# Attention's result stored token by token and turned by a transposing DMA, instead of by TensorE

## The chip, the cores and the metric

One Trainium2 chip, all 8 cores, one launch. Each core takes one of the 8 sequences of the batch with the whole weights; the cores exchange nothing. The metric is the device time of the slowest core, in microseconds.

## The reference

For each sequence of 2048 tokens and 4096 features:

```
x = x + layernorm(attention(layernorm(x)))       # w_in 6144 x 4096, w_out 4096 x 4096
x = x + layernorm(ffn(layernorm(x)))             # sign(weight) 4096 x 4096
```

Attention has 32 query heads and 8 key and value heads of 128 features, rotary embedding, a causal mask and a softmax over the keys; its result, 4096 features per token, is multiplied by `w_out.T`. The second part scales its input and output by a routing softmax over 8 experts and multiplies by the signs of the weights.

## The kernel before

The tokens are handled in four blocks of 512 (tb 0 to 3). An input of a projection lies in SBUF as a block of 128 partitions x 16384 bf16: partition p holds, for each of the 32 groups of 128 features, feature p of the group for 512 tokens. TensorE contracts over partitions, so every projection needs its input turned this way (features on partitions).

**The main line.** `main` walks through `groups`: v, k and q projections for blocks 0 and 1, then q, k and v for blocks 2 and 3, then the output projection ("o") for blocks 0 and 1 and for 2 and 3, then the second part ("f"). A pass of one group over one block is 128 matmuls of 512 columns, yielded in 32 steps of 4. The weights come by GpSimd's queue (`w_load`), 1 MB each, cast on the way, issued as the slot before comes free (`w_next`).

**The sides.** Generators are advanced beside the main line by its step number. Attention over blocks 0 and 1 ("att0") runs beside the q, k, v passes of blocks 2 and 3 (steps 802 to 1512); attention over blocks 2 and 3 ("att1") beside the output projection of blocks 0 and 1 (steps 1538 to 2040). "signs" (steps 802 to 1262) loads the second part's weights (`sgw`), turns them to signs and stores them (`wfs`). All engines work in program order, so this weaving is fixed.

**Attention.** An item is one head and one piece of 128 keys: `scores` makes a matmul into one of two PSUM banks taken in turn (`next_s`), ScalarE's exp reads it into `pt`; 3 items later `values` makes up to 4 matmuls of 129 columns into two banks. At the end of a head `scaled` divides by the sums (VectorE, into `an`: tokens on partitions, 4 x 128 features), and 3 items later `turned` takes a bank of `next_s`, makes 4 TensorE transposes of 128 x 128 (helper line 33) into it, VectorE copies the bank into one of three `ast` buffers (line 65), and the sync queue stores it to `As` in DRAM, 1 KB per partition. There are 128 heads in all (32 heads x 4 blocks).

**The queues around it.** The sync queue (SP) issues, in order: the q tiles' stores (`Qs<-qst`, two buffers, made by the rotary step on VectorE in the q passes), the q tiles' loads three heads ahead (`qb<-Qs`), the stores to `As`, the stores of signs (`wfs<-sgo`), and later `out2s<-o2a`, `x<-xin`, `o<-out2s`. `load_at(tb, over)` loads a block for the output projection from `As` in 4 DMAs of 1 MB (`blk_r<-As`). It is called at steps 1506, 1537, 2018 and 2050 for the blocks 0 to 3; their passes begin at the steps 1537, 1569, 2049 and 2081. A pass takes the quarters of the block in order, 8 steps each.

Of the kernel before, what the change touches and what calls it, by code (L numbers as in the profile page):

```python
# [7 lines left out]
BF16 = mybir.dt.bfloat16  # L8
# [6 lines left out]
E = 4096  # L15
# [12 lines left out]
def f_mm(out, lhsT, rhs, start=True, stop=True):  # L28
    return lambda e: e.matmul(out, lhsT, rhs, start=start, stop=stop)  # L29


def f_tr(out, in_, ident):
    return lambda e: e.transpose(out, in_, ident)  # L33
# [18 lines left out]
def f_tt(out, a, b, op):  # L52
    return lambda e: e.tensor_tensor(out, a, b, op=op)  # L53
# [10 lines left out]
def f_vcopy(out, in_):  # L64
    return lambda e: e.tensor_copy(out, in_)
# [21 lines left out]

def f_dma(out, in_):
    return lambda e: e.dma_start(out=out, in_=in_)  # L89


class Prog:
# [44 lines left out]
    def pe(self, make, waits=(), sig=False):  # L137
        return self.put("tensor", make, waits, "sT" if sig else None, 1)

    def act(self, make, waits=()):  # L140
        return self.put("scalar", make, waits, "sA", 1)

    def dve(self, make, waits=()):
        return self.put("vector", make, waits, "sV", 1)

    def load(self, eng, out, in_, name, waits=()):
        return self.put(eng, f_dma(out, in_), waits, name, 16)
# [49 lines left out]
def build_program():  # L197
    nc = bass.Bass("TRN2", target_bir_lowering=False)
    dt_in = lambda n, s, t: nc.dram_tensor(n, s, t, kind="ExternalInput").ap()
    scr = lambda n, s, t: nc.dram_tensor(n, s, t, kind="Internal").ap()  # L200
# [14 lines left out]
    out = nc.dram_tensor("out", [S, E], F32, kind="ExternalOutput").ap()  # L215

    Qs = scr("Qs", [4, 32, 128, 512], BF16)
    As = scr("As", [4, 128, 32 * 512], BF16)
    out2s = scr("out2s", [S, E], BF16)
    x2s = scr("x2s", [S, E], F32)  # L220
    ys = scr("ys", [1024, E], BF16)
# [3 lines left out]
    K = 1024  # L225
    BASE = 16512
    R0, R1, R2 = BASE, BASE + 32 * K, BASE + 64 * K
# [8 lines left out]
    al = nc.alloc_sbuf_tensor_at  # L236
# [14 lines left out]

    qb = [al(f"qb{i}", [128, 512], BF16, offset=R1 + i * K) for i in range(4)]
    pt = [al(f"pt{i}", [128, 512], BF16, offset=R1 + (4 + i) * K) for i in range(10)]
    an = [al(f"an{i}", [128, 512], BF16, offset=R1 + (14 + i) * K) for i in range(2)]
    rec = [al(f"rec{i}", [128, 4], F32, offset=R1 + (16 + i) * K) for i in range(2)]
    ast = [al(f"ast{i}", [128, 512], BF16, offset=R1 + (24 + i) * K) for i in range(3)]
    o2a = [al(f"o2a{i}", [128, 512], BF16, offset=R1 + (27 + i) * K) for i in range(4)]

    x5 = al("x5", [128, E], F32, offset=R1)
# [11 lines left out]
    o = F0  # L271

    def small(n, shape, t, nbytes):
        nonlocal o
        r = al(n, shape, t, offset=o)
        o += nbytes
        return r

    ident = small("ident", [128, 128], BF16, 256)
# [17 lines left out]
    o = p_end  # L297
# [6 lines left out]
    o = p_end + 2048  # L304
# [6 lines left out]
    p = Prog(nc)  # L311
    pe, act, dve, load = p.pe, p.act, p.dve, p.load
# [7 lines left out]
    def next_s():  # L320
        turn["s"] += 1
        return RB[(turn["s"] - 1) % 2]
# [260 lines left out]
    a_tok = {}  # L583
# [85 lines left out]
    LAG = 3  # L669
    pt_free = [[] for _ in pt]  # L670
    qb_free = [[] for _ in qb]
    an_free = [[], []]
    rec_free = [[], []]
    ast_free = [[] for _ in ast]
    as_tok = {}
    r1_over = [[]]
    att = {"pt": 0}
# [4 lines left out]
    def q_load(k):  # L682
        if k < len(heads):
            n = k % 4
            q_in[k] = load("sync", qb[n][:, :], Qs[heads[k][0], heads[k][1]], f"qb{n}",
                           [q_tok[heads[k]]] + qb_free[n] + r1_over[0])

    def attention(lo, hi):
        if lo == 0:
            for k in range(3):  # L690
                q_load(k)
        items = []
        for k in range(lo, hi):
            tb, h = heads[k]
            for kc in range(4 * tb + 4):
                items.append((k, tb, h, kc, max(0, kc - 4 * tb)))
        todo = {}
        made = {}
        norm = {}

        def scores(it):
            k, tb, h, kc, j = it
            qn = k % 4
            if kc == 0:
                q_load(k + 3)
            c0 = j * 128
            b = next_s()
            s = att["pt"] % len(pt)
            att["pt"] += 1
            ko = (h // 4) * 1024 + (kc % 8) * 128  # L710
            tk = pe(f_mm(b.f[:, c0:512], k_sb[kc // 8][:, ko:ko + 128], qb[qn][:, c0:512]),
                    [q_in[k]] + b.free + k_ready[kc // 8], sig=True)
            qb_free[qn] = [tk]
            col = tb * 32 + h
            ex = act(f_act(pt[s][:, c0:512], b.f[:, c0:512], AF.Exp, bias=qmx[:, col:col + 1], scale=ALPHA),
                     [tk] + pt_free[s] + nb_tok[tb] + r1_over[0])
            b.free = [ex]
            mk = ex
            if kc >= 4 * tb:
                mk = dve(f_tt(pt[s][:, c0:c0 + 128], pt[s][:, c0:c0 + 128], tri[:, :], ALU.mult),  # L720
                         [ex, tc[1]])
            made[k, kc] = (s, ex, mk)

        def values(it):

            k, tb, h, kc, j = it
            s, ex, mk = made.pop((k, kc))
            vo = ((kc % 8) * 8 + h // 4) * VN
            v = v_sb[kc // 8][:, vo:vo + VN]
            tk = None  # L730
            opened = set()
            for n in list(range(j + 1, 4)) + [j]:
                vb = VB[n // 2]
                first = kc == 0 and n // 2 not in opened
                opened.add(n // 2)
                w = [ex] + v_ready[kc // 8]
                if kc == 0:
                    w = w + vb.free
                if n == j:
                    w = w + [mk]  # L740
                tk = pe(f_mm(vb.f[:, (n % 2) * VN:(n % 2 + 1) * VN], pt[s][:, n * 128:(n + 1) * 128], v,
                             first, n % 2 == 1 and kc == 4 * tb + n), w, sig=(n == j))
            pt_free[s] = [tk]
            if kc - 4 * tb in (1, 3):
                scaled(k, (kc - 4 * tb) // 2, tk)

        def scaled(k, m, tk):
            vb = VB[m]
            v3 = vb.f[:, 0:2 * VN].rearrange("p (a b) -> p a b", b=VN)
            rc3 = rec[k % 2][:, 2 * m:2 * m + 2].unsqueeze(2)  # L750
            rc = dve(f_rcp(rc3, v3[:, :, 128:129]), [tk] + rec_free[k % 2])
            nv = dve(f_tt(an[k % 2][:, m * 256:(m + 1) * 256].rearrange("p (a b) -> p a b", b=128),
                          v3[:, :, 0:128], rc3.broadcast_to([128, 2, 128]), ALU.mult),
                     [tk, rc] + an_free[k % 2])
            vb.free = [nv]
            norm[k] = nv

        def turned(k):
            tb, h = heads[k]
            b = next_s()  # L760
            tk = None
            for n in range(4):
                tk = pe(f_tr(b.h[:, n * 128:(n + 1) * 128], an[k % 2][:, n * 128:(n + 1) * 128], ident[:, :]),
                        ([norm[k]] + b.free) if n == 0 else (), sig=(n == 3))
            an_free[k % 2] = [tk]
            rec_free[k % 2] = [norm[k]]
            n = k % 3
            ev = dve(f_vcopy(ast[n][:, :], b.h[:, 0:512]), [tk] + ast_free[n])
            b.free = [ev]
            st = load("sync", As[tb, :, h * 512:(h + 1) * 512], ast[n][:, :], f"as{n}", [ev])  # L770
            ast_free[n] = [st]
            as_tok[tb] = latest(as_tok.get(tb, []), [st])

        for n, it in enumerate(items):
            k, tb, h, kc, j = it
            at_n = n + LAG + max(0, 2 - kc)
            todo.setdefault(at_n, []).append(lambda it=it: values(it))
            if kc == 4 * tb + 3:
                todo.setdefault(at_n + 3, []).append(lambda k=k: turned(k))
        n = 0  # L780
        while n < len(items) or todo:
            if n < len(items):
                scores(items[n])
            for f in todo.pop(n, ()):
                f()
            yield 0.3 + (512 - items[min(n, len(items) - 1)][4] * 128) / 512
            n += 1
# [3 lines left out]

    def load_at(tb, over):
        b = blk[AB[tb]]
        a_tok["o", tb] = [[load("sync", b[:, c * 4096:(c + 1) * 4096], As[tb, :, c * 4096:(c + 1) * 4096],
                                f"at{tb % 2}{c}", as_tok[tb] + over)] for c in range(4)]


    x2_tok = {}
# [356 lines left out]
        r1_over[0] = xuse["x", 1]  # L1155

    def after_attention():
        r1_over[0] = p.now("sT", "sA", "sV", "as0", "as1", "as2", "o2a0", "o2a1", "o2a2", "o2a3")
        x5_free[0] = r1_over[0]
        o5_free[0] = r1_over[0]  # L1160
        f_over[0] = f_over[1] = p.now("sT")
        load_consts()
# [140 lines left out]
```

How the kernel before makes its waits and increments, by code:

```python
        def f(e, make=make, tgt=tgt, pairs=tuple(pairs)):  # L127
            for (h, v) in pairs:
                e.wait_ge(h, v)
            i = make(e)
            if tgt is not None:
                i.then_inc(*tgt)
# [19 lines left out]
    def wait(self, eng, toks):  # L152
        pairs = tuple((self.sem[t[0]][0], t[1]) for t in toks)
        self.q[eng].append(lambda e, pairs=pairs: [e.wait_ge(h, v) for (h, v) in pairs])
```

## Time and profile before

| | us |
|---|---|
| median of 3 runs | 4134.55 |
| the runs | 4120.65 to 4147.13 |
| the profiled execution's own time | 4127.55 |
| its span on the slowest core (core 6) | 4126.0 |
| spans of the 8 cores | 4091.9 to 4126.0 |

The profile is of core 6, one execution. PE is TensorE's matmuls, PEld its weight loads, DVE VectorE, ACT ScalarE, POOL GpSimd, SP the sync queue. A profile's row gives busy time; what bounds the kernel is read from what each engine waited for, in the stretch in question. On core 6, att0 runs from about 818 to 1690 us of the span and att1 from about 1720 to 2573 us.

### The profile page before, as it was taken

What the parts mean: (1) busy time and instruction counts of PE and PEld (TensorE: products, weight loads), DVE (VectorE), ACT (ScalarE), POOL (GpSimd) and SP (SyncE); (2) the same over time, 40 slices, a digit from 0 to 9 for tenths busy, and PEclk for the clock granted to TensorE, in tenths of its full rate; (3) what the DMA queues carried; (4) which work ended last, traced back from release to release, by engine and by line L of the source; (5) the groups of instructions that cost most, each with busy time, mean ns of one, the idle gap of its engine ahead of it and who ended that gap; (6) DMA issues with size and microseconds to landing.
All of it is one profiled execution on the core that took longest, in us unless ns stands there. A gap on an engine that the chain in (4) does not pass through costs nothing.

```text
span 4126.0 us, 61645 instructions; the slowest of 8 cores (4091.9 to 4126.0 us)
## 1 busy us (share of the span) xinstructions
PE 3870.7 (94%) x22113; PEld 1897.1 (46%) x22448; DVE 1722.9 (42%) x3284; ACT 1428.4 (35%) x2293; POOL 171.7 (4%) x327
## 2 busy tenths in 40 slices
PE   5999999988888999999999999989999999999997
PEld 2444444444444454555555555444444434344343
DVE  5155555755544453122211111334345666543444
ACT  2111111144555433366666666222212212121222
POOL 0000000000000000000000000000000000000110
PEclk8999999999999999999999999999999999999999
DMA  9445656588987834633332233885844534267874
GB/s 230 74 86 101 121 101 125 124 163 179 188 165 154 163 65 83 151 75 75 76 70 61 64 70 100 217 186 152 206 110 159 169 106 168 70 196 226 237 252 166
DMA packets 189945, 565.69 MB, mean 137 GB/s; under 512 B 21328, under 2 KB 96208, under 8 KB 160976
## 3 DMA queue, kind: packets, MB, share of 16 engines
q0 software_dynamic: 46512, 269.05, 34.5%
q1 hardware_dynamic: 143136, 292.68, 22.4%
q8 instruction: 187, 3.06, 0.3%
q14 instruction: 110, 0.90, 0.1%
HBM read 620.95 MB, written 142.61 MB: 185 GB/s over the span
## 4 chain that ended last, share of the span: by engine, by line
PE 76%; DMA 12%; DVE 5%; issue 3%; ACT 3%; SPq 1%; DVEq 0%; ACTq 0%; POOL 0%; POOLq 0%
PE ps L29 74%; DMA Qs<-qst 3%; DMA out<-xfc 3%; PE ps L33 2%; ACT pt L37 2%; DMA o<-out2s 2%; DMA wfs<-sgo 1%; DVE bn L77 1%; DMA x<-xin 1%; SPq L89 1%; DMA bia<-bias_in 1%; DMA wsl<-wv 1%; DVE yt L53 1%; DVE yst L53 1%; DVE t L53 0%
## 5 line engine op out<-in xcount | busy, mean ns | idle before, releaser
L29 PE MATMUL ps<-wsl,blk_r 128*128 128x512 bf16 x4982 | 1214.6, 384 | 47.6 <-DMA wsl<-wv 19.9
L29 PE MATMUL ps<-blk_r,wsl 128*128 128x512 bf16 x4986 | 1177.6, 383 | 12.6 <-DVE t L53 5.4
L37 ACT ACTIVATE pt<-ps,qmx 128x512 bf16<-128x512 f32 (+3 forms) x1280 | 763.0, 622 | 650.1 <-PE ps L29 640.3
L29 PEld LDWEIGHTS ps<-blk_r,wsl 128*128 128x128 bf16 x5120 | 494.1, 99 | 561.5 <-issue 24.0
L29 PEld LDWEIGHTS ps<-wsl,blk_r 128*128 128x128 bf16 x5120 | 478.0, 99 | 533.3 <-issue 78.1
L29 PE MATMUL ps<-qb,k_sb 128*128 128x512 bf16 (+3 forms) x1221 | 416.8, 347 | 65.1 <-ACT pt L37 49.0
L29 PE MATMUL ps<-wsg,blk_kv 128*128 128x512 fp8e4 x2048 | 470.6, 380 | 0.0
L29 PE MATMUL ps<-wsg,blk_r 128*128 128x512 fp8e4 x2048 | 457.2, 381 | 10.6 <-DVE yt L53 10.6
L29 PE MATMUL ps<-v_sb,pt 128*128 128x129 bf16 x4352 | 412.3, 222 | 13.1 <-DVE rec L73 5.1
L53 DVE TENSOR_TENSOR pt<-pt,tri 128x128 bf16<-128x128 bf16 x512 | 113.6, 225 | 697.0 <-ACT pt L37 684.8
L29 PEld LDWEIGHTS ps<-v_sb,pt 128*128 128x128 bf16 x4352 | 318.9, 98 | 140.3 <-issue 8.1
L29 PEld LDWEIGHTS ps<-wsg,blk_r 128*128 128x128 bf16 x2048 | 195.8, 98 | 255.0 <-issue 31.0
L29 PEld LDWEIGHTS ps<-wsg,blk_kv 128*128 128x128 bf16 x2048 | 188.5, 98 | 232.1 <-issue 28.8
L49 ACT CAST osb<-ps 128x512 bf16<-128x512 f32 x128 | 74.7, 585 | 466.4 <-PE ps L29 454.5
L53 DVE TENSOR_TENSOR t<-ps,sinb 64x512 f32<-64x512 f32 x320 | 220.5, 689 | 9.9
L29 PEld LDWEIGHTS ps<-qb,k_sb 128*128 128x128 bf16 x1280 | 125.3, 98 | 211.4 <-issue 111.7
L37 ACT ACTIVATE qsq<-qst 128x512 bf16<-128x512 bf16 x128 | 80.1, 625 | 378.8 <-DVE qst L53 377.4
L53 DVE TENSOR_TENSOR t<-ps,cosb 128x512 f32<-128x512 f32 x160 | 110.2, 689 | 238.6 <-PE ps L29 234.4
L77 DVE BATCH_NORM_STATS2 bn<-x 128x6 f32<-128x512 f32 x256 | 162.6, 682 | 57.4 <-DMA x<-xin 51.4
L37 ACT ACTIVATE mv<-mv,epsc 128x1 f32<-128x1 f32 x64 | 19.0, 297 | 414.4 <-DVE mv L81 414.4
L77 DVE BATCH_NORM_STATS2 bn<-o 128x6 f32<-128x512 bf16 x128 | 78.1, 679 | 180.8 <-DMA o<-out2s 180.8
L41 ACT ACTIVATE sgo<-sgw 128x1024 fp8e4<-128x1024 bf16 x128 | 134.1, 1047 | 51.3 <-DMA wfs<-sgo 42.7
(84 smaller groups left out, 2122.4 us busy)
## 6 DMA issues: line engine op xcount, KB each, us to landing
wsl<-wqk POOLq DMA_DIRECT2D x80, 1024.0 KB, 11.2
x<-xin SPq DMA_DIRECT2D x128, 512.0 KB, 8.7
wsl<-wout POOLq DMA_DIRECT2D x64, 1024.0 KB, 9.9
wsg<-wfs POOLq DMA_DIRECT2D x96, 512.0 KB, 5.2
sgw<-wffn POOLq DMA_DIRECT2D x32, 1024.0 KB, 14.1
x2s<-x SPq DMA_DIRECT2D x64, 512.0 KB, 4.0
wsl<-wv POOLq DMA_DIRECT2D x16, 1024.0 KB, 9.7
Qs<-qst SPq DMA_DIRECT2D x128, 128.0 KB, 7.4
```

The lines of the kernel that those rows point to most:

```text
L29: return lambda e: e.matmul(out, lhsT, rhs, start=start, stop=stop)
L33: return lambda e: e.transpose(out, in_, ident)
L37: return lambda e: e.activation(out, in_, func, bias=bias, scale=scale)
L41: return lambda e: e.activation(out, in_, AF.Sign, saturate=False)
L49: return lambda e: e.copy(out, in_)
L53: return lambda e: e.tensor_tensor(out, a, b, op=op)
L77: return lambda e: e.bn_stats(out, in_)
L89: return lambda e: e.dma_start(out=out, in_=in_)
```

## The change

`turned` becomes `stored`. The result of a head is stored as it lies in `an`, so `As` is now tokens x features: a store writes, for each of 128 partitions, 4 pieces of 128 features (256 bytes) into 4 different rows. `an` has four buffers instead of two, and a buffer is free when its store has landed. The block's loads become 4 transposing DMAs on the same queue, each of 512 tokens x 1024 features. TensorE's 4 transposes, the bank they took and VectorE's copy are gone. The store comes 1 item after the head's last values, not 3.

```diff
+def f_dmat(out, in_):
+    return lambda e: e.dma_start_transpose(out=out, in_=in_)
...
-    As = scr("As", [4, 128, 32 * 512], BF16)
+    As = scr("As", [4, 512, E], BF16)
...
-    an = [al(f"an{i}", [128, 512], BF16, offset=R1 + (14 + i) * K) for i in range(2)]
     rec = [al(f"rec{i}", [128, 4], F32, offset=R1 + (16 + i) * K) for i in range(2)]
-    ast = [al(f"ast{i}", [128, 512], BF16, offset=R1 + (24 + i) * K) for i in range(3)]
+    an = [al(f"an{i}", [128, 512], BF16, offset=R1 + (18 + i) * K) for i in range(4)]
...
-        def turned(k):
+        def stored(k):
             tb, h = heads[k]
-            b = next_s()
-            tk = None
-            for n in range(4):
-                tk = pe(f_tr(b.h[:, n * 128:(n + 1) * 128], an[k % 2][:, n * 128:(n + 1) * 128], ident[:, :]),
-                        ([norm[k]] + b.free) if n == 0 else (), sig=(n == 3))
-            an_free[k % 2] = [tk]
+            n = k % len(an)
+            st = load("sync", As[tb].rearrange("(a p) e -> p a e", p=128)[:, :, h * 128:(h + 1) * 128],
+                      an[n].ap().rearrange("p (a b) -> p a b", b=128), f"as{n}", [norm[k]])
+            an_free[n] = [st]
             rec_free[k % 2] = [norm[k]]
-            n = k % 3
-            ev = dve(f_vcopy(ast[n][:, :], b.h[:, 0:512]), [tk] + ast_free[n])
-            b.free = [ev]
-            st = load("sync", As[tb, :, h * 512:(h + 1) * 512], ast[n][:, :], f"as{n}", [ev])
-            ast_free[n] = [st]
             as_tok[tb] = latest(as_tok.get(tb, []), [st])
...
-                todo.setdefault(at_n + 3, []).append(lambda k=k: turned(k))
+                todo.setdefault(at_n + 1, []).append(lambda k=k: stored(k))
...
-        a_tok["o", tb] = [[load("sync", b[:, c * 4096:(c + 1) * 4096], As[tb, :, c * 4096:(c + 1) * 4096],
-                                f"at{tb % 2}{c}", as_tok[tb] + over)] for c in range(4)]
+        toks = []
+        for c in range(4):
+            d = b[:, c * 4096:(c + 1) * 4096].rearrange("p (a b) -> p a b", b=512)
+            toks.append([p.put("sync", f_dmat(d, As[tb, :, c * 1024:(c + 1) * 1024]),
+                               as_tok[tb] + over, f"at{tb % 2}{c}", 16)])
+        a_tok["o", tb] = toks
```

## Rows read from the trace of the kernel before

**Rows 1.** The page: busy per engine, 40 slices of the span, shares of the ending chain.
```profile
PE 3870.7 (94%) x22113; PEld 1897.1 (46%) x22448; DVE 1722.9 (42%) x3284; ACT 1428.4 (35%) x2293; POOL 171.7 (4%) x327
DMA  9445656588987834633332233885844534267874
PE 76%; DMA 12%; DVE 5%; issue 3%; ACT 3%; SPq 1%; DVEq 0%; ACTq 0%; POOL 0%; POOLq 0%
```
**Rows 2.** Windows: us, busy per engine, PE clock, DMA share, GB/s.
```profile
818.00:1150.00 332.00, 285.81 (x1675) 148.75 (x1707) 180.54 (x469) 160.74 (x251) 18.06 (x35) 0.93 0.86 174
1660.00:2090.00 430.00, 411.23 (x3023) 232.82 (x3081) 85.11 (x307) 258.69 (x440) 8.48 (x16) 1.00 0.38 89
2090.00:2580.00 490.00, 468.35 (x3563) 270.89 (x3627) 80.40 (x288) 323.10 (x541) 10.29 (x20) 1.00 0.34 76
```
**Rows 3.** Timeline of PE: start, us, instruction, count [idle before <- releaser].
```profile
1679.67 0.39 PE L33 MATMUL ps<-ident,an 128*128 128x128 bf16 x4
1679.89 0.85 PE L29 MATMUL ps<-v_sb,pt 128*128 128x129 bf16 x12
...
1902.26 0.38 PE L33 MATMUL ps<-ident,an 128*128 128x128 bf16 x4 [0.20 <-ACT pt L37]
```
**Rows 4.** Groups by form in 818:2580: busy, mean ns | idle before, what ended it.
```profile
L33 PE MATMUL ps<-ident,an 128*128 128x128 bf16 x512 | 49.9, 220 | 30.7 <-ACT pt L37 22.7 <-DVE pt L53 7.4 <-DVE an L53 0.5
L65 DVE COPY ast<-ps 128x512 bf16<-128x512 bf16 x128 | 54.2, 424 | 143.8 <-PE ps L33 143.1 <-issue 0.6
```
**Rows 5.** PE's waits in 1660:2090, then 2090:2580: us, times, longest.
```profile
PE ps L33 <- ACT pt L37: 9.2, 21, 0.7
PE ps L33 <- ACT pt L37: 7.8, 16, 0.7
```
**Rows 6.** DMA view of 842:870 and, last two rows, of 872:878: packets, MB, share of 16 engines.
```profile
q0 software_dynamic: 595, 4.35, 94.1%
q1 hardware_dynamic: 594, 0.54, 7.5%
...
q1 hardware_dynamic: 1261, 1.54, 72.9%
q0 software_dynamic: 20, 0.07, 6.0%
```
**Rows 7.** DMA view of 0:3 (pieces of 256 bytes), then 1740:1756 (of 1 KB), then 1690:1698 (of 8 KB).
```profile
q1 hardware_dynamic: 254, 0.06, 8.7%
q1 hardware_dynamic: 532, 0.48, 9.0%
q1 hardware_dynamic: 336, 2.49, 100.6%
```
**Rows 8.** Chain of waits: start, us, what.
```profile
842.04 29.30 DMA Qs<-qst
918.42 33.04 DMA Qs<-qst
```
**Rows 9.** DVE's waits in 818:1150, then in 1150:1400: us, times, longest.
```profile
DVE qst L53 <- DMA Qs<-qst: 42.5, 6, 12.7
DVE qst L53 <- DMA Qs<-qst: 31.5, 4, 12.5
```
**Rows 10.** Timeline of the sync and GpSimd queues around the four block loads.
```profile
1686.92 3.15 SPq L89 DMA_DIRECT2D blk_r<-As  x4
1701.47 0.53 POOL L89 DMA_DIRECT2D wsl<-wout  x1 [6.38 <-PE ps L29]
1719.78 1.91 SPq L89 DMA_DIRECT2D blk_r<-As  x4
1769.05 0.32 SPq L89 DMA_DIRECT2D out2s<-o2a  x1
2534.97 2.96 SPq L89 DMA_DIRECT2D blk_r<-As  x4
2580.62 3.12 SPq L89 DMA_DIRECT2D blk_r<-As  x4
2590.92 2.36 SPq L89 DMA_DIRECT2D x<-xin  x4
2602.44 5.77 SPq L89 DMA_DIRECT2D out2s<-o2b  x4
```
**Rows 11.** Chain after the fourth load, and (timeline) the matmul that waited at its end.
```profile
2593.32 25.06 DMA o<-out2s
...
2638.96 1.01 PE L33 MATMUL ps<-ident,o 128*128 128x128 bf16 x8 [7.06 <-DVE o L57]
```

More of the change, by code:

```diff
@@ L671, in build_program @@
     qb_free = [[] for _ in qb]
-    an_free = [[], []]
+    an_free = [[] for _ in an]
     rec_free = [[], []]
-    ast_free = [[] for _ in ast]
     as_tok = {}
@@ L751, in scaled @@
             rc = dve(f_rcp(rc3, v3[:, :, 128:129]), [tk] + rec_free[k % 2])
-            nv = dve(f_tt(an[k % 2][:, m * 256:(m + 1) * 256].rearrange("p (a b) -> p a b", b=128),
+            nv = dve(f_tt(an[k % len(an)][:, m * 256:(m + 1) * 256].rearrange("p (a b) -> p a b", b=128),
                           v3[:, :, 0:128], rc3.broadcast_to([128, 2, 128]), ALU.mult),
-                     [tk, rc] + an_free[k % 2])
+                     [tk, rc] + an_free[k % len(an)])
             vb.free = [nv]
             norm[k] = nv
-        def turned(k):
+        def stored(k):
             tb, h = heads[k]
-            b = next_s()
-            tk = None
-            for n in range(4):
-                tk = pe(f_tr(b.h[:, n * 128:(n + 1) * 128], an[k % 2][:, n * 128:(n + 1) * 128], ident[:, :]),
-                        ([norm[k]] + b.free) if n == 0 else (), sig=(n == 3))
-            an_free[k % 2] = [tk]
-            rec_free[k % 2] = [norm[k]]
-            n = k % 3
-            ev = dve(f_vcopy(ast[n][:, :], b.h[:, 0:512]), [tk] + ast_free[n])
-            b.free = [ev]
-            st = load("sync", As[tb, :, h * 512:(h + 1) * 512], ast[n][:, :], f"as{n}", [ev])
-            ast_free[n] = [st]
+            n = k % len(an)
+            st = load("sync", As[tb].rearrange("(a p) e -> p a e", p=128)[:, :, h * 128:(h + 1) * 128],
+                      an[n].ap().rearrange("p (a b) -> p a b", b=128), f"as{n}", [norm[k]])
+            an_free[n] = [st]
+            rec_free[k % 2] = [norm[k]]
             as_tok[tb] = latest(as_tok.get(tb, []), [st])
@@ L1157, in after_attention @@
     def after_attention():
-        r1_over[0] = p.now("sT", "sA", "sV", "as0", "as1", "as2", "o2a0", "o2a1", "o2a2", "o2a3")
+        r1_over[0] = p.now("sT", "sA", "sV", "as0", "as1", "as2", "as3", "o2a0", "o2a1", "o2a2", "o2a3")
         x5_free[0] = r1_over[0]
```

## The prediction

> **What bounds the kernel now.** I read the page first [rows 1]: PE is busy for 94% of the span, and 76% of the chain that ended last is PE. What takes PE's time away makes the kernel shorter, where PE is what the stage waits for. The windows show where that holds [rows 2]: in att1 (1660 to 2580) PE is busy for 411 of 430 and 468 of 490 us at full clock, with DMA at 0.38 and 0.34. In the first part of att0 (818 to 1150) it is not so clean: PE 286 of 332 us, clock 0.93, DMA share 0.86. There the chain runs through q tiles' stores that took 29 and 33 us [rows 8], and VectorE, waiting for such a store's buffer, stood 42.5 + 31.5 = 74 us in 10 waits up to 1400 [rows 9]. So the change has to be read as two stages: in one PE's work is the price, in the other a DMA queue is.
>
> **PE's transposes: -29.4 us.** In the timeline the 4 transposes of a head start at 1679.67 and the next values at 1679.89 [rows 3]: 0.22 to 0.23 us a head. The row's 220 ns each [rows 4] is latency of overlapping instructions and would give four times too much. 128 heads x 0.23 = 29.4 us, all on PE's own line.
>
> **The bank they took: -17.0 us.** A transpose had to wait until the exp before had left the bank: 9.2 us in 21 waits and 7.8 us in 16 in att1 [rows 5], as in the third line of [rows 3]. Without it the next user of that bank is the next score matmul, one step of the main line later, when the exp is done. The bounds are 0 (the wait moves there whole) and 17.0; I take 17.0, since values and about a microsecond of the main line's matmuls lie between. The rest of the 30.7 us before transposes [rows 4] stood in the stalls of the first stage, which end by a DMA; I count nothing of it.
>
> **VectorE's copies: 0.** 54.2 us [rows 4] go from an engine that is busy for 85 of 430 us in att1 [rows 2]; PE's wait was for exp, not for it. In the first stage the copy held VectorE while it waited for the transposes (143 us over both stages), beside a PE that was busy; 0 again, at best a few us.
>
> **The stores: 0 by time, +20 us by turns.** A store now makes 512 pieces of 256 bytes instead of 128 of 1 KB: 32 per DMA engine instead of 8. The nearest rows give 8.7% x 16 x 3 us / 254 = 16 ns for a piece of 256 bytes (a read) and 9.0% x 16 x 16 / 532 = 43 ns for one of 1 KB [rows 7]. A store then takes between 32 x 16 = 0.5 and 32 x 43 = 1.4 us of each engine, against 0.34 now. In att1 that is nothing at a DMA share under 0.4. But between 842 and 870, with weights queued by GpSimd, the two queues made 595 and 594 packets [rows 6]: they take turns one for one, and a turn lasts 0.941 x 16 x 28 / 595 = 0.71 us for a weight packet and 0.06 for one of ours. A store's 8 packets and its signal are 9 turns or 6.9 us; with 33 turns it is 25 us, 18 more, and the q tiles' stores and loads issued behind it on the same queue wait that long. What limits this is that the wait ends when the weights are through: from 872 the sync queue made 1261 packets in 6 us beside 20 [rows 6], and the store issued at 842.04 landed at 871.34 [rows 8], just when that began. It could not have come much later with longer queues before it. So each of the 10 waits grows by between 0 and 18 us; I take 2, near the lower end because the row shows the end fixed by the weights, which gives +20; the end of 18 gives +180. The q tiles' loads come three heads ahead, some 20 us here, and go the same way; they are in the same 20. `an` has 4 buffers at one head in about 7 us, so a landing within 28 us costs nothing.
> The page "DMA: Bandwidth & Descriptors" of the Trainium skill (Specifications) speaks against this part: it wants 512 bytes for line rate and says that below it the engine reads, modifies and writes. No row of before writes 256-byte pieces. By that page a store would cost about twice the bytes' time, an estimate of 1 us a store and no more on the path in att1.
>
> **The block loads: +5 us.** A block is 16384 pieces of 256 bytes (one token's part of one group of 128 features), if the transposing DMA moves such pieces: 1024 per engine. At 16 ns that is T = 17 us a block, at 43 ns T = 44; a plain block of 8 KB pieces takes 4.19 MB at the 2.49 MB in 8 us of [rows 7], 13 us. I take 17, since the piece is of that row's size. The covers [rows 10]: the first block is issued at 1686.9 and its pass begins when the next one's load is released, at 1719.8 (33 us); the second has until the pass ends at 1769.0 (49 us); the third from 2535.0 until 2580.6 (45 us); the fourth from 2580.6 to about 2608 (27 us); and each further quarter has 7 us more. With T = 17 no pass waits. The first is shared with weights from 1694.6 on, every 6.9 us (four of them, the second shown) [rows 10]: 57% of it is through before, and between two weights of about 5 us there are 2 us free, so it ends at about 1724, in time for the last quarter at 1740. The sync queue may be held while the pieces are made: the q load behind the second block is three heads or some 33 us early, so nothing waits. Only behind the fourth block is something due: `x<-xin` at 2590.9, then `o<-out2s`, landed at 2618.4, on which PE finally stood 7.06 us [rows 11]. Every us by which T exceeds 13 goes there: +5 with some issue time.
>
> **Sum.** -29.4 - 17.0 + 20 + 5 = -21 us against the execution's own 4127.55. The median of the runs is 7 above that; I put the same difference to it: 4134.55 - 21 = 4113.
>
> **Rivals.**
> *A, the turns cost nothing.* The four pieces of a partition may go in one turn, or the end of the weights releases everything as it does now. For it: the landing at 871.34. Against: 595 to 594, for packets of 1 KB, which were single pieces. Then -46 + 5 and perhaps a few us of VectorE's time: 4090, faster by a little over 1%.
> *B, the sync queue starves in att0 (slower).* Place: the weights' backlogs between 818 and 1400. A store to `As` that enters before the q tiles' stores blocks them from the beginning of the backlog, and the wait starts earlier, instead of ending later. Price: up to 18 us in each of 10 waits, 4134.55 - 41 + 180 = 4274. It cancels the gain from 4 us a wait on and is slower by 1% from 8 us on. Against: q stores come between with two buffers, and while PE stands no new weights are asked for.
> *C, the transposing DMA is slow (slower).* With T = 44 the first block is late by about 11 us and the fourth pushes `o<-out2s` by 31: +42 in place of +5, 4150. From T = 58 it is slower by 1%. As a mechanism: blocks that turn at a rate of a single 128 x 128 at a time exceed every cover, and the loads follow each other on one queue.
> The page "VectorE: DVE Perf Modes" (The three transpose paths) gives 1309 ns for 128 x 128 by DMA against 390 ns by TensorE; here four by TensorE took 0.23 us in line. One after another, 128 of them would be an estimate of 168 us a block and, less the covers, about 430 us in all: near 4540. I give that 3 in 100, within C, because several are surely in flight.
> *D, the gain is off the path.* PE's 46 us turn into waits for exp (ACT 259 of 430 and 323 of 490 us busy [rows 2]): about 4134. Against: 60 to 66% is not a bound.
>
> **How the numbers follow.** This kernel's measurement tells about 1% (41 us) from no change. Forecast (within 1%) 0.42, with a range of its own of 4095 to 4140; A 0.27 (faster); B 0.12 and C 0.11 (slower); D 0.08 (within 1%). Faster 0.27, same 0.50, slower 0.23. The range must take in A, both ends of T up to 44 and some of B: 4078 to 4200 leaves out the rest of B and C, under 0.2.
>
> **What would show it.** In the profile after: no L33 on `an`, no `ast`; att1 (from its block load to the last store) shorter by about 70 x 0.23 + 17 = 33 us; no wait of score matmuls in their place. `Qs<-qst` landings near 30 us as before in number and length, and VectorE's waits for them at 74 to 95 us; B would show them above 150, and landings of `As<-an` above 25 us in the backlogs. `blk_r<-As` landing within 20 us of its issue where no weights flow; C would show PE waiting for it at the start of the first pass, or longer than 12 us on `DVE o`. I am wrong if the stage from 818 to 1400 moves by more than 40 us either way.

## The result and the profile after

The changed kernel takes 4225.9 us in the median of 4 runs (4203.09 to 4398.41), against 4140.84 for the kernel before on the same chip; ratio 1.0202 (95% interval 1.0166 to 1.0238): slower by about 85 us, clear of no change and outside the predicted range. Its profiled execution took 4232.04 us, 104 us more than that of before; the profile is again of core 6. Ratios leave out executions in which the cores of one die were slowed; where too few were left for a ratio (x2, x6, x7 at first), the single times stand instead.

The page, against [rows 1]: busy time per engine, the busy tenths of PE in 40 slices and its granted clock in the same slices, the chain, and the group in which PE's new idle time stands (busy, mean ns of one | idle before it):

```profile
PE 3834.6 (91%) x21609; PEld 1871.0 (44%) x21936; DVE 1672.4 (40%) x3156; ACT 1427.5 (34%) x2293; POOL 171.1 (4%) x327
...
PE   5999999968888899779999999499999999999797
...
PEclk8999999989999999889999999799999999999999
...
PE 72%; DMA 14%; SPq 6%; DVE 3%; issue 2%; ACT 2%; DVEq 0%; ACTq 0%; POOL 0%; POOLq 0%
...
L29 PE MATMUL ps<-wsl,blk_r 128*128 128x512 bf16 x4999 | 1220.8, 385 | 111.2 <-DMA blk_r<-As 64.7
```

The same two rows before:

```profile
PE   5999999988888999999999999989999999999997
...
PEclk8999999999999999999999999999999999999999
```

PE is busy for 36 us less and stands 140 us more. SPq, the sync queue as a link of the chain, rose from 1% to 6%, and PE falls to 7 tenths in the slices 17 and 18 (1692 to 1904 us) and to 4 tenths in slice 26, where before it was at 9. The granted clock falls with it: while PE stands again and again, it is 0.70 between 1750 and 1807 us and 0.76 between 1807 and 1850, where before it is 1.00 from 1687 to 2535. PE's waits over the whole run say for what it stood:

```profile
PE ps L29 <- DMA blk_r<-As: 64.7, 5, 28.2
PE ps L29 <- DMA qb<-Qs: 56.2, 4, 18.1
PE ps L29 <- ACT pt L37: 53.7, 43, 18.2
PE ps L33 <- DVE o L57: 31.1, 4, 27.7
PE ps L29 <- DVE yt L53: 30.5, 4, 20.1
PE ps L29 <- DVE pt L53: 25.2, 25, 14.6
```

The first two rows did not exist before. This is core 6; on the cores 0 and 3 PE stood 48.6 and 28.3 us for the weights (`wsl<-wout`) and never for the block. The sync queue's timeline around the loads (start, us), against [rows 10]:

```profile
1719.30 88.10 SPq L93 DMA_TRANSPOSE blk_r<-As  x4
...
1832.01 1.34 SPq L89 DMA_DIRECT2D qb<-Qs  x2
...
2581.87 46.46 SPq L93 DMA_TRANSPOSE blk_r<-As  x4
...
2643.17 30.62 SPq L93 DMA_TRANSPOSE blk_r<-As  x4
2674.10 27.68 SPq L89 DMA_DIRECT2D x<-xin  x4
2701.83 0.43 SPq L89 DMA_DIRECT2D o<-out2s  x1
```

Before, four block loads held the queue for 2 to 3 us; now the first block's hold it for 88 us, and the second's start only then, at 1807.7. The q loads that came at 1721.8 come at 1832.0.

Following one event after the other in the two traces gives the ledger of core 6 (time after less time before): first store of att0 -6; first block's load issued +32 (1719.3 against 1686.9); second block's load +88 (1807.7 against 1719.8); first store of att1 +100; third block's load +47 (2581.9 against 2535.0); fourth +63; next stage's first `x<-xin` +83; end +104. So att0 lost 38 us, the loads of the first two blocks 68, then 53 came back, and the loads of the other two with what stands behind them took 36. The 68 and the 53 do not measure PE: the first store of att1 stands behind both blocks' loads on the queue, and is late with them. Of the 15 us between first and third block's load (+32 to +47) the experiments separate the gain and the loss below.

### The profile page after: what moved, and what is told of

It is laid out like the page before. It is cut to its first block, busy times and chain, and to the rows that moved or that the text cites. A ratio compares the mean times of both kernels' runs of the same rounds, so it can differ in the third digit from the quotient of the medians.

```text
span 4230.5 us, 60454 instructions; the slowest of 8 cores (4122.1 to 4230.5 us)
## 1 busy us (share of the span) xinstructions
PE 3834.6 (91%) x21609; PEld 1871.0 (44%) x21936; DVE 1672.4 (40%) x3156; ACT 1427.5 (34%) x2293; POOL 171.1 (4%) x327
## 4 chain that ended last, share of the span: by engine, by line
PE 72%; DMA 14%; SPq 6%; DVE 3%; issue 2%; ACT 2%; DVEq 0%; ACTq 0%; POOL 0%; POOLq 0%
PE ps L29 71%; DMA out<-xfc 5%; SPq L93 4%; DMA wfs<-sgo 3%; DMA qb<-Qs 2%; DMA Qs<-qst 2%; SPq L89 1%; PE ps L33 1%; DMA x<-xin 1%; ACT pt L37 1%; DMA bia<-bias_in 1%; DVE t L53 1%; DMA wsl<-wv 1%; DVE bn L77 1%; DVE yt L53 0%
## 5 line engine op out<-in xcount | busy, mean ns | idle before, releaser
L29 PE MATMUL ps<-wsg,blk_r 128*128 128x512 fp8e4 x2048 | 458.1, 382 | 30.5 <-DVE yt L53 30.5
```

## The experiments

**x7: no turning at all.** It asks what the removal alone is worth.

```
-    As = scr("As", [4, 512, E], BF16)
+    As = scr("As", [4, 128, 32 * 512], BF16)
-            st = load("sync", As[tb].rearrange(...)[:, :, h * 128:(h + 1) * 128], ...)
+            st = load("sync", As[tb, :, h * 512:(h + 1) * 512], an[n][:, :], f"as{n}", [norm[k]])
-            toks.append([p.put("sync", f_dmat(d, As[tb, :, c * 1024:(c + 1) * 1024]), ...)])
+            toks.append([load("sync", b[:, c * 4096:(c + 1) * 4096], As[tb, :, c * 4096:(c + 1) * 4096], ...)])
```

> Before without the turning alone: no transposes, no VectorE copy; the result is stored in 1 KB pieces and loaded plainly. It leaves out the turning of attention's result, so its output is another one. Theory 1 (the gain is real and lies on PE's line; the whole loss is in DMA): as far below before as att1 was shorter in the change (first store of att1 to third block load, 53 us) plus 15 to 25 us in att0: 65 to 80 us below before, ratio 0.981 to 0.985. Rival (the 53 us are catching up after the late first block, not a gain): only the 46 us of the prediction, ratio 0.989, or less.

Its times are 4087.85 and 4080.66 us; run again:

> The kernel without any turning once more, for its ratio: 0.986 to 0.991, as its two undisturbed runs (4087.85 and 4080.66 us) had it. The output leaves out the turning.

Ratio 0.9893 (0.9851 to 0.9935), 44 us. Theory 1's 65 to 80 us are wrong and the rival is right: part of the change's 53 us in att1 was catching up after a late start. The gain lies between the first and the third block's load: 848.0 to 848.1 us on the eight cores before, 805.3 to 805.6 in x7. Att0 gave nothing (the table behind x5).

**x1: the change with plain loads.** The new load reads the same bytes as 128 partitions of 8 KB.

```
+        src = As[tb].rearrange("(p r) e -> p (r e)", r=4)
-            toks.append([p.put("sync", f_dmat(d, As[tb, :, c * 1024:(c + 1) * 1024]), ...)])
+            toks.append([load("sync", b[:, c * 4096:(c + 1) * 4096], src[:, c * 4096:(c + 1) * 4096], ...)])
```

> The change with its block loads made plain DMAs of 8 KB pieces; the stores keep their 256-byte pieces. It leaves out the turning, so its output is another one. Theory 1 (the transposing loads cost about 110 us, the stores about 47 us in att0): 0.994 of before, 25 us below it (85 - 110), and att0 as long as in the change (start of attention to the first block load 883 us against 845 before). Rival (the small pieces of the stores are the main loss, also behind the loads): still 1.01 or more.

Ratio 0.9953 (0.9932 to 0.9975), as Theory 1 had it (0.994). From the first store to the first block load att0 takes 880 us (835.1 to 1715.5), in x7 848 (836.6 to 1684.8), before 845. So the transposing loads cost 1.0202 - 0.9953, about 100 us, and the stores' small pieces some 30 us in att0 (25 us by the ratios of x1 and x7).

**x2: before, with the transposing loads alone.**

```
+        src = As[tb].rearrange("p (r e) -> (p r) e", r=4)
-        load("sync", b[:, c * 4096:(c + 1) * 4096], As[tb, :, c * 4096:(c + 1) * 4096], ...)
+        p.put("sync", f_dmat(d, src[:, c * 1024:(c + 1) * 1024]), ...)
```

> Before with nothing changed but the block loads, which are the change's transposing DMAs of 512 rows x 1024 features from the same bytes; TensorE still turns the result, so it is turned twice and the output is another one. Theory 1 (each block's transposing load costs 55 to 60 us beside weights, about 110 us in all four): ratio 1.024 to 1.028; first block's four DMAs hold the sync queue for over 80 us. Rival (the loads are slow only because the stores' small pieces and q loads crowd the same queue): ratio under 1.01.

Its time is 4222.43 us, 87 us over the median of the ten of before beside it (4135): 1.021, a little under the expected 1.024. No second one stands beside it, but its first block shows the same thing with 1 KB stores on the queue:

```profile
1683.93 105.43 SPq L93 DMA_TRANSPOSE blk_r<-As  x4
```

On the other cores it is 52 to 93 us. The rival (the loads are slow for the small stores) is out.

**x5: the change without the weights beside the loads.**

```
     def w_load(g, c, free):
+        if g in (24, 32):
+            w_tok[g, c] = w_tok[g - 1, c]
+            return
```

> The change, and the 8 weight loads (of 64 for the output projection) that run beside the first and the third block's transposing loads are left out; the passes use the weights that lie in the slots, so the output is another one. All else is the change. Theory 1 (a transposing DMA beside GpSimd's weight loads takes turns with them and loses its rate; alone it takes about 6.3 us a quarter): first block's four DMAs hold the sync queue for about 26 us instead of 88, PE waits for blk_r under 10 us instead of 65, and the time is 60 to 85 us below the change, ratio to before 1.000 to 1.006. Rival (the transposing DMA is slow by itself, whatever runs beside): the ratio stays above 1.015.

Ratio 0.9951 (0.9930 to 0.9972): the same as with plain loads, and better than the 1.000 to 1.006 expected, since the loads' whole cost is gone. The first block's four (start, us), then the DMA view of 1715:1738 (packets, MB, share of 16 engines):

```profile
1714.12 20.26 SPq L93 DMA_TRANSPOSE blk_r<-As  x4
```
```profile
q1 hardware_dynamic: 16517, 4.20, 86.1%
```

4.20 MB in 23 us. The change itself, between 1745 and 1800, one of its transposing DMAs beside weights:

```profile
q1 hardware_dynamic: 2056, 0.52, 76.2%
q0 software_dynamic: 403, 2.92, 41.7%
```

2056 pieces of 256 bytes in 55 us, where x5 moved 16517 in 23; and the weights, too, go at 2.92 MB in 55 us, 53 GB/s, where in [rows 6] they had 4.35 MB in 28 us, 155 GB/s. Both streams fall to a third or less, while the engines' share says that they are busy. This is no sharing of time.

Three stretches between fixed points of the program, smallest to largest of the 8 cores, us:

| | before | x7 | x1 | x5 | the change |
|---|---|---|---|---|---|
| first `sgw` load (start of att0) to first block's load | 844 to 865 | 847 to 867 | 880 to 895 | 871 to 899 | 870 to 898 |
| first to third block's load | 848.0 to 848.1 | 805.3 to 805.6 | 805.3 to 805.5 | 805.3 to 805.5 | 833 to 874 |
| third block's load to the end | 1577 to 1591 | 1575 to 1596 | 1577 to 1595 | 1575 to 1600 | 1582 to 1651 |

The second row is the whole gain, 43 us on every core, and x5 keeps it with transposing loads exactly as x1 does with plain ones. On core 6 of the change it takes 862.6, 57 more than in x5: PE's new waits for the block and for a q tile are 51 of them, and the rest fits the lowered clock.

**x10: the same weights in small DMAs.**

```
+        if g in (24, 32):
+            for q in range(4):
+                cs = slice(q * 1024, (q + 1) * 1024)
+                w_tok[g, c] = load("gpsimd", chunk(g, c)[:, cs], w_source(g, c)[:, cs], ...)
+            return
```

> The change, with the 8 weight loads that run beside the first and third block's transposing DMAs cut into four DMAs of 1024 columns each (2 KB pieces in SBUF instead of 8 KB). Output the reference's. Theory 1a (a big weight packet holds an engine, and all 16 engines have to come to the same tile, so the cost goes with the packets' size): the stretch with both streams shortens, first block's DMAs 40 to 60 us instead of 70 to 100, ratio 1.005 to 1.012. Theory 1b (the cost goes with the number of changes between the streams, or with the bytes): no shorter, or longer, ratio 1.018 or more.

Ratio 1.0115 (1.0076 to 1.0153). The first block's DMAs (start, us):

```profile
1707.74 54.83 SPq L93 DMA_TRANSPOSE blk_r<-As  x4
```

Over the 8 cores the first block takes 53 to 60 us in this run and 62 to 103 us in the change. So the same bytes in smaller packets cost less, as Theory 1a had it. Its reason, that engines wait for each other at a tile, fits but is not shown: no run shows the tile itself, nor whether GpSimd's queue or the cast matters. At the third block the two runs overlap (24 to 41 us here, 22 to 59 in the change).

**x4: the loads of blocks 0 and 2 quarter by quarter, earlier.** Each quarter of a block's load goes out when that quarter of the old block was last read, which is before the next weights are asked for.

```
-    at(1506, lambda: load_at(0, xuse["x", 2]))
-    at(2018, lambda: load_at(2, xuse["o", 0]))
+    for c in range(4):
+        at(1480 + 8 * c, lambda c=c: load_at(0, xuse["x", 2], [c]))
+        at(1992 + 8 * c, lambda c=c: load_at(2, xuse["o", 0], [c]))
```

> The change, with the first and the third block's four transposing DMAs issued one by one, each when its quarter of the old block has been read for the last time (steps 1480, 1488, 1496, 1504 and 1992, 2000, 2008, 2016), so that they run before the weight loads that ran beside them. The output is the reference's. Theory 1 (beside weights a transposing DMA loses its rate, alone it takes 6 to 7 us a quarter): PE waits for blk_r under 10 us instead of 65, the ratio falls from 1.020 to 0.997 to 1.004. Rival (what costs is the sync queue held by the DMAs, whenever it is): the ratio stays above 1.010, with waits for qb in place.

Ratio 1.006 (1.0023 to 1.0096): 60 us of the loss gone, 0.002 short of the expected span. The first block's DMAs now take 5 to 6 us each. The second block, no longer held back, met the last weight load:

```profile
1704.01 14.47 SPq L93 DMA_TRANSPOSE blk_r<-As  x2
...
1740.59 50.95 SPq L93 DMA_TRANSPOSE blk_r<-As  x4
1791.66 1.01 SPq L89 DMA_DIRECT2D qb<-Qs  x2
```

and PE waited 20.3 us for a q tile behind it (the other 37.4 us of such waits stand in att0, as the change's 38.1 do). That is the rival's price, but by the slowed load, not by the queue as such: x5, with 18 to 22 us of hold, has no wait for a block or a q tile there on any core.

**x3: the stores in 1 KB pieces.** With `As` as before, 128 source rows of 4096 columns turn into the same block.

```
-            d = b[:, c * 4096:(c + 1) * 4096].rearrange("p (a b) -> p a b", b=512)
-            ... f_dmat(d, As[tb, :, c * 1024:(c + 1) * 1024])
+            d = b[:, c * 4096:(c + 1) * 4096].rearrange("p (a b) -> p a b", b=128)
+            ... f_dmat(d, As[tb, :, c * 4096:(c + 1) * 4096])
```

> The change with the stores in 1 KB pieces: As keeps the layout of before (128 partitions x 16384, a head's 512 elements of a partition together), and a transposing DMA reads 128 rows x 4096 columns of it, in 32 groups of 128 columns, which lands as the same block. The output is the reference's. Theory 1 (256-byte pieces take turns with weights and cost 31 us of att0): start of attention to the first block load falls by 25 to 40 us to that of the run without any turning (848 us), the loads' cost stays, ratio 1.010 to 1.015. Rival (the stores' pieces are not the cause, but that they leave earlier or hold `an` longer): att0 stays at 883 us and the ratio at 1.020.

Ratio 1.0167 (0.999 to 1.0344), too wide to tell it from the change by the time. The stage does: from the first store to the first block's load it takes 851 us (835 to 1686), against 883; over the 8 cores 808 to 851 against 856 to 883. VectorE's wait for q stores in att0 is 108.6 us in x3 and 137.1 in the change, PE's for q loads 18.4 and 38.1.

**x6 and x8: both together.**

> Both of the kernels above together, output the reference's. If the two costs add (Theory 1): 1.020 - 0.020 - 0.008 = 0.992, 30 to 35 us under before, with about 12 to 20 us left behind the fourth block. If the rest of the costs is common to both (rival): 0.998 or more.

> The kernel above with the fourth block's load called at step 2059 instead of 2050, behind the first loads of the next stage (x and out2s rows for the layer norms) on the sync queue. Output the reference's. Theory 1 (the transposing DMAs, 26 us, delay o<-out2s, on which PE then stands for some 28 us): PE's wait for DVE o falls from about 28 to 7 us and the time by 10 to 20 us more, ratio 0.988. Rival (the fourth block is then late itself): PE waits for blk_r instead and nothing is gained.

x6's times are 4131.35 and 4136.27 us. x8's one edit (2050 to 2059) did not change the order that it aimed at, because a side begins one step after its start; it is x6 once more, and gave 0.9983 (0.9937 to 1.0029). The expected 0.992 was missed by the second block, 52 us beside a weight load, and by the fourth, behind which PE stood 32.9 us for `DVE o`:

```profile
1705.28 52.49 SPq L93 DMA_TRANSPOSE blk_r<-As  x4
...
2553.16 32.36 SPq L93 DMA_TRANSPOSE blk_r<-As  x4
2585.83 1.85 SPq L89 DMA_DIRECT2D x<-xin  x4
```

In the stretch below a single 1 MB load is in flight beside the first of the four, which took 38.1 us and ended as that load landed (16 to 38 us on the 8 cores). So one load can be enough. In x8's 1722:1742:

```profile
q1 hardware_dynamic: 1337, 0.34, 116.8%
q0 software_dynamic: 47, 0.34, 12.0%
```

47 weight packets in 20 us, where [rows 6] has 595 in 28.

**x9: kept apart.**

```
-    at(1537, lambda: load_at(1, xuse["x", 3]))
+    at(1545, lambda: load_at(1, xuse["x", 3] + [w_tok[24, 3]]))
-    at(2050, lambda: load_at(3, xuse["o", 1]))
+    at(2060, lambda: (load_at(3, xuse["o", 1] + [w_tok[32, 3]]), load_consts()))
-        load_consts()            # in after_attention
+        cst["g"] = load("gpsimd", ..., r1_over[0] + a_tok["o", 3][3])
```

> The kernel with early quarters and 1 KB stores, and no transposing DMA left beside a GpSimd load: the second block's load is called at step 1545 instead of 1537 and waits for the last weight load before it; the fourth block's load is called at step 2060, behind the next stage's first x and out2s loads on the sync queue (the run x8_order meant this, but its step 2059 still came ahead of them), and waits for the last weight load; the three small constants' loads wait for the fourth block. Output the reference's. Theory 1 (any GpSimd load beside a transposing DMA slows both until the load is through; nothing else of it costs): every block's four DMAs take 24 to 30 us, PE's wait for qb at the second block (22 us) goes, that for DVE o (33 us) falls to about 8, ratio 0.986 to 0.991, 50 to 55 us under before. Rival (the sync queue held for 26 us costs as much by itself): 0.995 or more.

Ratio 0.9905 (0.9881 to 0.9929), 39 us under before and some 120 under the change; it leaves nothing out and is the fastest such kernel here. The sync queue, and PE's waits:

```profile
2548.07 2.36 SPq L89 DMA_DIRECT2D x<-xin  x4
2550.48 0.89 SPq L89 DMA_DIRECT2D o<-out2s  x1
2551.47 26.49 SPq L93 DMA_TRANSPOSE blk_r<-As  x4
```
```profile
PE ps L29 <- DMA qb<-Qs: 16.7, 4, 7.2
PE ps L33 <- DVE o L57: 16.4, 5, 11.8
```

Of the wait for a block 0.7 us is left, and between 2540 and 2680 PE no longer waits for `DVE o` at all (the 11.8 us stand later); it stands 6.1 us for the weights that now come later and 5.7 for ScalarE's `o2b` instead. x7, which turns nothing, is at 0.9893, within the intervals. x9 also has another order of loads, which x7 has not (PE's waits for `DVE o` from 2500 to 2800 us are 12 to 19 us on x7's cores and 10 to 13 on x9's), so a cost of some 5 us could hide there, and before in x9's order was not run. The cleaner pair is x5 and x1, in the same order: kept apart from GpSimd's loads, the transposing DMAs cost nothing that these runs can tell.

## Why the prediction was wrong

**PE's transposes and their bank, -46.4 us: the sum right, in part by luck.** x7 measured 44 us by its ratio, but not where it was forecast. Between first and third block's load 43 us went, and att0, which was to give 15, gave nothing: there the stretch is 844 to 865 us before and 847 to 867 in x7. The sync queue took it back: PE stood 14 to 20 us there for q loads in x7, 0 to 4 before. The bank's 17.0 us came out at 16.8 (core 1, PE's waits between first and third block's load, before, then x7):

```profile
PE ps L33 <- ACT pt L37: 16.8, 36, 0.7
PE ps L29 <- ACT pt L37: 11.5, 56, 0.5
...
PE ps L29 <- ACT pt L37: 11.2, 55, 0.5
```

The first row is gone and the other did not grow. The 26 us left over 62 heads are 0.41 us a head, where 0.23 was read from two starts in the timeline. So the term was some 10 us too small in att1 and 15 too large in att0.

**VectorE's copies, 0: right.** DVE fell from 1722.9 to 1672.4 us and nothing more than the 46 us moved.

**The stores, +20 us: right in mechanism, too small.** It is +30 us (att0 in x1 against x7). The turns are there: the DMA view of the change in the same window as [rows 6] has again one of ours for one of theirs, with half the bytes:

```profile
q0 software_dynamic: 606, 4.44, 98.1%
q1 hardware_dynamic: 641, 0.27, 5.0%
...
As<-an SPq DMA_DIRECT2D x2, 128.0 KB, 28.6
```

Stores landed in 28.6 us there (median of two), forecast 25; the two of before in that window took 24.0, so little was added. VectorE's waits for q stores in att0 went from 74 us in 10 to 137.1 in 12, 5 us a wait and not the 2 I took; the 137.1 lie between the 95 of the forecast and the 150 set for rival B. PE waited 38.1 us for q loads, which the term had within its 20. It also waited 18.9 us for `an`, but not for want of buffers: VectorE stood 23.3 us for a q store's buffer just then, and `rec` and `an` came behind that in its program. No core waited for a landing of `As<-an`, though the longest took 39.3 us, so the four buffers were enough. Of 1 KB stores (x7) the wait for q stores is 106.4 us, too, without att0 being longer; so that wait alone is a poor measure. Rival B had the place right and was over by far: 180 us.

**The block loads, +5 us: this step failed.** Its text ran: "With T = 17 no pass waits", and of the first block "57% of it is through before, and between two weights of about 5 us there are 2 us free, so it ends at about 1724." (By the times given there it is 7.7 of 17 us, 45%; that changes nothing here.) Two things were wrong. Alone, a block takes 20 to 24 us and not 17 (x5, first block, from its issue to its last landing, 8 cores); that was within my bounds and cost nothing that x5 can tell. But I treated the two queues as sharing time, from rows that show only plain DMAs taking turns. Beside GpSimd's loads, a transposing DMA and the loads both fall to a fraction of their rate: 62 to 103 us for the first block, 100 us over all (the change against x1). No row of before could show it, and my upper bound, T = 44, was taken from a piece's cost on an unshared queue. Rival C had the right sign and place with the wrong cause: the DMA is not slow, it is slow in company.
The Trainium skill gives in "Advanced Engine Details and Errata" (X-Bar Transpose (TRN2)) "TRN2 transpose DMAs are as fast as regular DMAs". Here the third block landed in 20 to 24 us in x5 against 13 to 16 for the plain one before, and the first took 62 to 103 beside weights; the measurement decides. The 1309 ns per 128 x 128 that the Trainium skill gives in "VectorE: DVE Perf Modes" (The three transpose paths) would be an estimate of 168 us a block one after another; measured 20 to 24.

**"The q load behind the second block is three heads or some 33 us early, so nothing waits": wrong.** It came 110 us later than before, 78 beyond the 32 us by which the stage was late anyway, and PE waited 18.1 us for it. The hold follows from the slow load. Of the hold by itself x5 and x9, at 19 to 22 us for the second block, show no wait for a q tile there.

**The fourth block: right place, wrong size.** PE's wait for `DVE o` went from 7.06 to 27.7 us; in x9, with the order changed and the streams apart, it is gone there.

**Open.** In the last stage PE's wait for `DVE yt` is 30.5 us on the change's page and 10.6 before. Over the 8 cores it is 9 to 30 us in the change, 2 to 12 before, 4 to 17 in x1 and 3 to 19 in x5; the page is of the slowest core, so part of this is which core was slowest. Nothing was changed there, and it was not tested. Also open is why the same company costs so unlike: in x8 one weight load made a transposing DMA take 16 to 38 us, while in the change's third block, on the cores 3 and 4, one weight load made it 8.5 us and the block 22.

## What to carry to other kernels

A transposing DMA can take over TensorE's transposes at no cost that these runs can tell, if no other queue's large loads run in the same time; the gain comes only where TensorE bounds the stage. Issue it when its destination's part comes free, and make it wait for the last load before it. Before moving work onto a queue, count its pieces and not its bytes, and look at what is queued behind it. An operation that the trace does not have needs one run beside the traffic that it will meet; bounds from rows of other operations on idle queues do not hold it.

## What the runs showed of the hardware

- A transposing DMA and one weight load of 1 MB, in flight together, can slow each other: 47 weight packets in 20 us (x8) against 595 in 28 us beside plain DMAs. Weights in DMAs of a quarter of the size made it milder at the first block (53 to 60 us against 62 to 103), not harmless.
- Alone, four transposing DMAs (4.2 MB) held the sync queue for 18 to 21 us and landed 20 to 24 us after the first was issued (x5, first block, 8 cores).
- A transposing DMA of 1 MB holds the sync queue for 5.5 us when alone (median of x5), a plain one for 0.3 to 1.8.
- Beside a backlog of weights, stores in 256-byte pieces make even the issue of the next plain DMA slow (sync queue of the change, start and us):

```profile
924.18 6.64 SPq L89 DMA_DIRECT2D qb<-Qs  x1
930.92 6.25 SPq L89 DMA_DIRECT2D Qs<-qst  x1
937.25 5.63 SPq L89 DMA_DIRECT2D As<-an  x1
```

The same three kinds took 0.3 us in most cases before. Some issues are slow with 1 KB stores too, but less: the longest of a q load in att0 was 18.2 us in the change and 5.5 in x7.
